# Filler matmuls on TensorE ahead of the last tiles of three layer norms

## The chip, the cores and the metric

One NeuronCore of one Trainium2 chip runs the program. The metric is the device time of one execution, in microseconds (us). TensorE (PE in the profile) multiplies, VectorE (DVE), ScalarE (ACT) and GpSimd (POOL) work on the data around it, and SyncE (SP) issues the loads.

## What is computed

Two layers, each a cross attention and then a mixture of experts, each behind a layer norm without weights and each added to the running x. There are 8 sequences of 56 tokens, 448 tokens of width 256, and a context of 8 x 1500 rows.

```python
x = x + _L0_xattn_ref(_layernorm(x), ctx_2048, ...)   # softmax attention, 16 heads of 128, 4 key heads
x = x + _L0_ffn_ref(_layernorm(x), ...)               # 8 experts of 176, top 2, and a shared one of 352
x = x + _L1_xattn_ref(_layernorm(x), ctx_2048, ...)   # linear attention: relu features of q and k, 16 heads of 16
x = x + _L1_ffn_ref(_layernorm(x), ...)               # 8 experts of 176, top 2, and a shared one of 704
```

## The kernel before

The program has three stages. `sums_and_queries` and `softmax_attention` fill the first 1046 us: they go through the context once for the key and value sums of the second layer and once for the softmax attention of the first. The third stage, `tail`, does everything that works on the 448 tokens, and the change lies in it alone.

In `tail` the tokens stand as four tiles of 112 (`TT` is 4, `TP` is 112), token by row, in `x`. One PSUM tensor, `bank`, has eight banks of 512 words. Each engine has its own list of instructions, written out by hand; semaphores order them across engines. The order on TensorE, with the lines that the prediction names:

1. `wo.turn_sums` and four calls of `wo.spread` (L1312): the softmax sums are spread over all partitions. One call is 8 matmuls. The weights of each are one column of `pick`, read 128 times (`pick[:, n:n + 1].to_broadcast([128, 128])`), the moving operand is `stack`, 128 x 112.
2. `wo.project`, four tiles (L102 to L104), with `ln1.turn` (L1213) of the tile before behind each. `turn(t)` waits for `xn_done`, transposes the two halves of one normalised tile and is read by ScalarE (`high` L1229, `copy` L1243), then by VectorE (`low` L1236).
3. `moe0.logits` (L1489: 16 instructions with 8 moving columns), then `moe0.tensor`: for each block of 128 hidden units `widen` (12 matmuls of 448 columns, L102 to L104), `spread` (L1524), `narrow` (L102 to L104, 256 columns). After two blocks TensorE turns the router's result (`turn_weights` L1512) and waits until ScalarE and VectorE have split it.
4. `ln2.turn` for four tiles, the queries (`lin.query` L1766) and features (L1779) of the linear attention, then `lin.read` (L1791: 16 instructions for one sequence, with 34 moving columns), `lin.turn` (L1803) and `lin.project` (L1815), with `ln3.turn` of the tile two back behind each.
5. `ln3.turn` of the last two tiles, `moe1.logits` (L1489) and `moe1.tensor`, built as in 3.

Behind `lin.project` VectorE adds the result to `x` (`lin.add` L1866, semaphore `lin.added`), takes mean and variance (L1173 to L1180), ScalarE computes a first reciprocal root (L1187, L1190), and VectorE sharpens it and writes the normalised tile into `scratch` (L1206, semaphore `xn_done`). ScalarE runs `ln3.guess` of tile 3 ahead of `high` and `copy` of tiles 2 and 3. `logits` of tile 0 waits until all four tiles went through `low`.

Of the kernel before, what the change touches and what calls it, by code (L numbers as in the profile page):

```python
# [18 lines left out]
TT = 4  # L19
TP = NTOK // TT  # L20
# [1862 lines left out]
def tail(nc, a, out, ident, kv, qT, qT_at, rz):  # L1883
# [8 lines left out]
    with ExitStack() as ctx:  # L1892
        p = Phase(nc, ctx, "tail")
        units = E * EU + SHARED1
        bank = p.ps("bank", [128, 8, 512])
# [24 lines left out]
        ln1, ln2, ln3 = (Norm(nc, p, f"ln{i}", x, xnT, xn, scratch, bank, banks, ident, zero)  # L1920
                         for i, banks in ((1, (6, 7, 0, 2)), (2, (0, 1, 2, 3)), (3, (0, 1, 2, 3))))
# [3 lines left out]
        wo = AttentionOutput(nc, p, x, qT, rz, a["wo0"], bank, ident)  # L1925
        lin = Readout(nc, p, kv, ln2, bank, ident, zero)
# [8 lines left out]
        @block.sync  # L1935
        def _(sp):
            wo.load(sp)
            sp.dma_start(x[:], a["x"].rearrange("(t p) d -> p t d", p=TP)).then_inc(x_loaded, 16)
            moe0.load_router(sp, a["router0"])
            moe1.load_router(sp, a["router1"])  # L1940
            moe0.load(sp, a["gate0"], a["up0"], a["down0"])
            lin.load(sp, room, a["wq1"], a["bq1"], a["wqf"], a["wo1"], a["bo1"])
            sp.wait_ge(moe0.w_lo, 3 * moe0.blocks)
            moe1.load(sp, a["gate1"], a["up1"], a["down1"])
            for t in range(TT):
                sp.wait_ge(moe1.added, t + 1)
                sp.dma_start(out[t * TP:(t + 1) * TP, :], x[:, t, :]).then_inc(stored, 16)
            sp.wait_ge(stored, 16 * TT)

        @block.tensor  # L1950
        def _(pe):
            wo.turn_sums(pe)
            for b in range(4):
                wo.spread(pe, b)
            for t in range(TT):
                for i in range(4):
                    wo.project(pe, t, i)
                    if t == 0 and i == 3:
                        wo.spread(pe, 4)
                        wo.spread(pe, 5)  # L1960
                    if t == 1 and i == 1:
                        wo.spread(pe, 6)
                        wo.spread(pe, 7)
                if t >= 1:
                    ln1.turn(pe, t - 1)
            pe.wait_ge(wo.scaled, 2 * B)
            ln1.turn(pe, TT - 1)
            for t in range(TT):
                moe0.logits(pe, t)
            moe0.tensor(pe)  # L1970
            for t in range(TT):
                ln2.turn(pe, t)
            lin.query(pe)
            lin.features(pe)
            for b in range(4):
                lin.read(pe, b)
            for t in range(TT):
                lin.turn(pe, t)
                lin.project(pe, t)
                if t + 2 < TT:  # L1980
                    lin.read(pe, 2 * t + 4)
                    lin.read(pe, 2 * t + 5)
                if t >= 2:
                    ln3.turn(pe, t - 2)
            for t in range(TT - 2, TT):
                ln3.turn(pe, t)
            for t in range(TT):
                moe1.logits(pe, t)
            moe1.tensor(pe)
# [213 lines left out]
```

## Time and profile before

| what | value |
|---|---|
| median of 3 runs | 1308.1 us (1306.59 to 1308.49) |
| the profiled execution, its own time | 1307.69 us |
| its span in the trace | 1306.0 us |
| busy: PE, DVE, ACT, POOL | 92%, 68%, 56%, 41% of the span |
| mean granted TensorE clock over the span | 0.963 of full speed |
| `tail`, from 1046 us to the end | 260 us |

The granted clock has two levels here: 1.00 is 2.4 GHz, 0.50 is 1.2 GHz. A row of the time line gives the start, how long the group was busy, engine, line, operation and tile, shape, and in brackets the idle time of that engine ahead of it and who ended it. In a time line a matmul's own duration holds its latency too; in a row that stands for a run of matmuls, the duration divided by the count is close to the step from one to the next. In the chain of waits a piece is only the part of the work that the end of the kernel had to wait for.

### The profile page before, as it was taken

The page shows a single profiled execution, that of the slowest core. Times are in us where ns is not written, and L with a number is a line of the kernel's source. Part 1 is how long each engine was busy: PE and PEld are TensorE (multiplying, and loading weights), DVE is VectorE, ACT ScalarE, POOL GpSimd, SP SyncE. Part 2 cuts the span into 40 slices and gives each one's busy share as a digit, 9 for nine tenths or more (in the row PEclk, how much of TensorE's full clock was granted, in tenths as well). Part 3 has the DMA queues.
Part 4 walks back from the last instruction along what each step waited for, and adds up shares of the span by engine and source line. Part 5 has one row for each costly group of instructions (what it writes and reads, how often), then busy time and mean ns, then how long its engine had stood idle before and what let it go on. Part 6 is the DMA issues. An engine that isn't in the chain of part 4 may idle for free. (4 is left out here: it accounts for less than half of the span.)

```text
span 1306.0 us, 27038 instructions
## 1 busy us (share of the span) xinstructions
PE 1199.6 (92%) x9589; PEld 1044.7 (80%) x9589; DVE 884.8 (68%) x1829; ACT 732.5 (56%) x1285; POOL 538.6 (41%) x559
## 2 busy tenths in 40 slices
PE   5999999999879999999999999999999876997798
PEld 4888888889758888888788887888878776785586
DVE  5666656566657887878887788778886465555554
ACT  4656556556545666576665666666656433442443
POOL 2423232232225363553545535445364063562242
PEclk9999999999988999999999999999999967997799
DMA  4211111110031111011110111101000070022000
GB/s 144 69 42 56 39 34 53 39 39 1 2 90 53 48 48 48 1 47 47 47 47 0 47 47 34 60 0 47 0 1 1 1 246 20 2 115 86 1 1 15
DMA packets 38795, 56.04 MB, mean 43 GB/s; under 512 B 3106, under 2 KB 37202, under 8 KB 38226
## 3 DMA queue, kind: packets, MB, share of 16 engines
q1 hardware_dynamic: 37922, 54.23, 13.1%
q10 hardware_dynamic: 816, 1.05, 0.3%
q8 instruction: 36, 0.59, 0.2%
q14 instruction: 21, 0.17, 0.0%
HBM read 54.81 MB, written 0.46 MB: 42 GB/s over the span
## 5 line engine op out<-in xcount | busy, mean ns | idle before, releaser
L1118 POOL TENSOR_TENSOR att_sq<-att_work,att_sq 128x500 fp32r<-128x500 f32 x90 | 119.8, 1331 | 159.7 <-DVE att_sq L1018 159.7
L1122 POOL TENSOR_TENSOR attention_kk<-att_work,attention_kk 128x500 fp32r<-128x500 f32 x90 | 122.1, 1357 | 153.3 <-DVE attention_kk L1026 153.3
L102 PE MATMUL att_csum<-att_pT,att_cn 125*128 125x448 f32 x384 | 156.3, 407 | 5.1 <-DVE att_pT L1067 4.4
L944 ACT ACTIVATE att_pr<-att_pr,att_nmx 112x1500 f32<-112x1500 f32 (+1 forms) x96 | 108.5, 1130 | 72.4 <-DVE att_nmx L1055 72.4
L104 PE MATMUL att_csum<-att_pT,att_cn 125*128 125x448 f32 x384 | 141.1, 367 | 0.0
L103 PE MATMUL att_csum<-att_pT,att_cn 125*128 125x448 f32 x384 | 140.0, 365 | 0.0
L535 DVE SCALAR_TENSOR_TENSOR attention_kk<-kvs_keys_ps,kvs_bk,attention_kk 64x500 fp32r<-64x500 f32 x96 | 70.8, 738 | 91.7 <-ACT attention_kk L419 90.1
L1067 DVE TENSOR_TENSOR att_pT<-att_ring,att_pT 125x448 fp32r<-125x448 f32 x192 | 118.3, 617 | 21.7 <-ACT att_pT L960 21.5
L1052 DVE TENSOR_SCALAR_CACHE_REDUCE att_pr<-att_ring 112x500 f32<-112x500 f32 x192 | 121.8, 675 | 6.4 <-PE att_ring L104 5.0
L290 PE MATMUL kvs_feat<-kvs_f,attention_kk 128*125 128x256 f32 x768 | 113.0, 284 | 10.9 <-DVE kvs_kp L607 10.1
L877 PEld LDWEIGHTS att_ring<-all_ident,att_pr 112*125 112x125 f32 x768 | 110.9, 190 | 14.4 <-ACT att_pr L944 2.2
L419 ACT ACTIVATE attention_kk<-kvs_keys_ps,kvs_bk 64x500 fp32r<-64x500 f32 x96 | 64.8, 675 | 92.3 <-PE kvs_keys_ps L104 91.0
L960 ACT ACTIVATE att_pT<-att_ring 125x448 fp32r<-125x448 f32 x192 | 102.5, 534 | 23.7 <-PE att_ring L877 23.7
L877 PE MATMUL att_ring<-all_ident,att_pr 112*125 112x112 f32 x768 | 111.6, 272 | 1.8 <-ACT att_pr L944 1.8
L290 PEld LDWEIGHTS kvs_feat<-kvs_f,attention_kk 128*125 128x125 f32 x768 | 98.5, 186 | 16.0 <-issue 14.1
L933 ACT ACTIVATE att_work<-att_proj,att_eps 128x500 f32<-128x500 f32 x90 | 60.8, 676 | 86.5 <-PE att_proj L104 86.5
L1021 DVE TENSOR_TENSOR att_work<-att_proj,att_work 128x500 f32<-128x500 f32 x90 | 60.9, 677 | 55.8 <-ACT att_work L940 55.4
L102 PE MATMUL att_ring<-attention_kk,attention_q 128*112 128x500 f32 x192 | 77.8, 405 | 17.5 <-DVE att_pr L1052 12.2
L472 ACT ACTIVATE kvs_kp<-kvs_feat,kvs_zero 125x512 f32<-125x512 f32 x96 | 65.9, 687 | 42.9 <-PE kvs_feat L290 42.4
L938 ACT ACTIVATE att_work<-att_mean,att_eps 128x500 f32<-128x500 f32 x90 | 61.1, 678 | 45.3 <-PE att_mean L835 45.3
L102 PEld LDWEIGHTS att_csum<-att_pT,att_cn 125*128 125x128 f32 x384 | 73.2, 191 | 15.1 <-DVE att_pT L1067 9.6
L1018 DVE CAST att_sq<-att_work 128x500 fp32r<-128x500 f32 x90 | 51.6, 574 | 39.8 <-ACT att_work L933 39.7
(279 smaller groups left out, 3276.9 us busy)
## 6 DMA issues: line engine op xcount, KB each, us to landing
attention_raw_t<-in_ctxT SPq DMA_DIRECT2D x45, 500.0 KB, 4.0
att_raw_n<-in_ctx SPq DMA_DIRECT2D x16, 750.0 KB
tail_gate_w<-in_gate SPq DMA_DIRECT2D x1, 2112.0 KB, 8.1
tail_up_w<-in_up SPq DMA_DIRECT2D x1, 2112.0 KB, 13.9
kvs_raw_q<-in_wq SPq DMA_DIRECT2D x8, 256.0 KB, 4.0
tail_wo_raw<-in_wo SPq DMA_DIRECT2D x4, 512.0 KB, 6.9
tail_down_w<-in_down SPq DMA_DIRECT2D x1, 2048.0 KB, 18.0
tail_gate_w<-in_gate SPq DMA_DIRECT2D x1, 1760.0 KB, 12.0
```

Source lines behind the costliest of these rows:

```text
L102: nc.tensor.matmul(out, w_lo, x_hi, start=start, stop=False, skip_group_check=True)
L103: nc.tensor.matmul(out, w_hi, x_lo, start=False, stop=False, skip_group_check=True)
L104: return nc.tensor.matmul(out, w_hi, x_hi, start=False, stop=stop, skip_group_check=True)
L290: last = nc.tensor.matmul(feat[0:KP, half, z], ks[:, c, 2 * half + g, y], f2[:, w, :], start=(w == 1), stop=(w == 0), skip_group_check=True)
L535: nc.vector.scalar_tensor_tensor(ks[64:128, c, 2 * m + h, :], keys_ps[y, 0:CH], bk[y, m:m + 1], ks[0:64, c, 2 * m + h, :].bitcast(F32), AL ...
L877: last = nc.tensor.transpose(ring[0:KP, t % 3, j * TP:(j + 1) * TP], pr[:, j, t * KP:(t + 1) * KP], ident[0:TP, 0:TP])
L944: nc.scalar.activation(pr[:, j, keys], pr[:, j, keys], ACT.Exp, scale=-1.0, bias=nmx[:, j:j + 1], accum_out=z[:, 4 * u + j, c:c + 1]).then ...
L960: nc.scalar.activation(pT[0][:, t % 3, :], ring[0:KP, t % 3, 0:QU], ACT.Copy).then_inc(pT_hi, 1)
L1052: nc.vector.tensor_scalar(pr[:, j, c * CH:(c + 1) * CH], ring[0:TP, c, 0:CH], -1.0, 3.0e38, ALU.mult, ALU.min, accum_out=mn[:, j, c:c + 1] ...
L1067: nc.vector.tensor_tensor(pT[1][:, t % 3, :], ring[0:KP, t % 3, 0:QU], pT[0][:, t % 3, :].bitcast(F32), ALU.subtract).then_inc(ring_free, 1)
L1118: nc.gpsimd.tensor_tensor(sq[1][:, i % 2, :], work[:, i % 2, :], sq[0][:, i % 2, :].bitcast(F32), ALU.subtract).then_inc(sq_lo, 1)
L1122: nc.gpsimd.tensor_tensor(kk[:, c, 2 + gi, :], work[:, i % 2, :], kk[:, c, gi, :].bitcast(F32), ALU.subtract).then_inc(k_lo, 1)
```

## The change

A helper `steady(n, count)` issues `count` equal matmuls into bank `n`, 112 columns each, with the operands of `wo.spread`: the first column of `pick`, read 128 times, and `stack`. Nobody reads the result, and no semaphore is raised. It is called four times on TensorE: 36 matmuls ahead of the last tile of the first norm, 44 ahead of the four tiles of the second, and 10 and 16 ahead of tiles 2 and 3 of the third. Ahead of the 10 TensorE waits until `lin.added` is 4, the number of tiles.

```diff
         @block.tensor
         def _(pe):
+            def steady(n, count):
+                for _ in range(count):
+                    nc.tensor.matmul(bank[:, n, 0:TP], wo.pick[:, 0:1].to_broadcast([128, 128]),
+                                     wo.stack[:], start=True, stop=True, skip_group_check=True)
+
             wo.turn_sums(pe)
...
             pe.wait_ge(wo.scaled, 2 * B)
+            steady(3, 36)
             ln1.turn(pe, TT - 1)
             for t in range(TT):
                 moe0.logits(pe, t)
             moe0.tensor(pe)
+            steady(7, 44)
             for t in range(TT):
                 ln2.turn(pe, t)
...
-            for t in range(TT - 2, TT):
-                ln3.turn(pe, t)
+            pe.wait_ge(lin.added, TT)
+            steady(7, 10)
+            ln3.turn(pe, TT - 2)
+            steady(7, 16)
+            ln3.turn(pe, TT - 1)
             for t in range(TT):
                 moe1.logits(pe, t)
             moe1.tensor(pe)
```

How the order on TensorE changes at the first norm, between the end of the attention's projection and the router's logits of the first mixture (- before, + changed):

```order
 L104 MATMUL tail_bank<-tail_wo_7144,tail_o_7146 112x256
-L1213 MATMUL tail_bank<-all_ident,tail_scratch 128x112 x4
+L1213 MATMUL tail_bank<-all_ident,tail_scratch 128x112 x2
+L1954 MATMUL tail_bank<-tail_stack,tail_pick 128x112 x36
+L1213 MATMUL tail_bank<-all_ident,tail_scratch 128x112 x2
 L1489 MATMUL tail_bank<-tail_moe_router,tail_xnT 112x8 x8
```

The 36 matmuls stand between the transposes of tile 2 and those of tile 3. They have no wait of their own but the one on `wo.scaled`, which stood there already.

The same at the third norm, behind the last projection of the linear attention:

```order
 L1815 MATMUL tail_bank<-tail_lin_wo,tail_attT 112x256 x2
-L1213 MATMUL tail_bank<-all_ident,tail_scratch 128x112 x6
+L1213 MATMUL tail_bank<-all_ident,tail_scratch 128x112 x2
+L1954 MATMUL tail_bank<-tail_stack,tail_pick 128x112 x10
+L1213 MATMUL tail_bank<-all_ident,tail_scratch 128x112 x2
+L1954 MATMUL tail_bank<-tail_stack,tail_pick 128x112 x16
+L1213 MATMUL tail_bank<-all_ident,tail_scratch 128x112 x2
 L1489 MATMUL tail_bank<-tail_moe_router,tail_xnT 112x9 x8
```

Here 10 matmuls and the new wait stand ahead of the transposes of tile 2, and 16 ahead of those of tile 3; the transposes of tile 1 keep their place. The other engines' lists are unchanged.

## Rows read from the trace of the kernel before

**Rows 1.** The page's second part: TensorE's granted clock in 40 slices.
```profile
PEclk9999999999988999999999999999999967997799
```

**Rows 2.** Chain of waits in the tail: start us, us, engine, tile, line.
```profile
1104.39 3.12 PE tail_bank L1489 x16
...
1181.33 5.22 PE tail_bank L1766 x8
...
1189.90 4.34 PE tail_bank L1791 x64
...
1214.41 0.42 DVE tail_scratch L1206
...
1214.88 0.65 PE tail_bank L1213 x2
...
1216.79 3.13 PE tail_bank L1489 x16
```

**Rows 3.** Stretches of the tail: from:to, length, PE busy (count), PEclk, DMA share, GB/s.
```profile
1048.20:1055.10 6.90, 6.90 (x32) 0.50 1.02 306
...
1097.20:1099.90 2.70, 0.00 (x0) 1.00 0.57 140
1100.10:1110.20 10.10, 6.41 (x26) 0.50 0.06 20
1114.20:1116.50 2.30, 0.00 (x0) 1.00 0.00 0
1117.20:1120.40 3.20, 3.20 (x9) 0.50 0.00 0
1175.20:1185.20 10.00, 5.62 (x14) 0.50 0.84 286
...
1192.20:1198.90 6.70, 6.10 (x47) 0.50 0.01 2
1199.10:1209.10 10.00, 7.72 (x76) 1.00 0.00 1
1209.30:1222.80 13.50, 7.28 (x28) 0.50 0.01 2
```

**Rows 4.** Time line of PE: the spreading of the softmax sums, at either clock.
```profile
1048.14 7.08 PE L1312 MATMUL tail_bank<-tail_stack,tail_pick 128*128 128x112 f32 x32 [1.50 <-DVE tail_stack L1357]
...
1068.60 1.89 PE L1312 MATMUL tail_bank<-tail_stack,tail_pick 128*128 128x112 f32 x16
1070.33 0.33 PE L102 MATMUL tail_bank<-tail_wo,tail_o 128*112 128x256 f32 x1
```

**Rows 5.** Time line of PE at the first norm, and behind it.
```profile
1102.51 0.61 PE L1213 MATMUL tail_bank<-all_ident,tail_scratch 112*128 112x112 f32 x2 [5.36 <-DVE tail_scratch L1206]
...
1108.27 0.57 PE L104 MATMUL tail_bank<-tail_xn,tail_wide 128*128 128x448 f32 x1
...
1111.20 0.37 PE L102 MATMUL tail_bank<-tail_xn,tail_wide 128*128 128x448 f32 x1
```

**Rows 6.** Time line of PE and DVE at the second norm, and reading at full clock.
```profile
1179.00 1.75 PE L1213 MATMUL tail_bank<-all_ident,tail_scratch 112*128 112x112 f32 x8 [5.55 <-DVE tail_scratch L1206]
...
1178.54 1.39 DVE L1206 TENSOR_SCALAR tail_scratch<-tail_x,tail_ln_mv,tail_ln_rstd 112x256 f32<-112x256 f32 x4
...
1180.80 0.39 DVE L1249 COPY tail_xnT<-tail_bank 128x224 f32<-128x224 f32 x1 [0.35 <-PE tail_bank L1213]
...
1201.81 1.84 PE L1791 MATMUL tail_bank<-tail_kvd,tail_qf 128*56 128x34 f32 x32
```

**Rows 7.** Time line of PE, DVE and ACT at the third norm.
```profile
1208.01 0.41 PE L1213 MATMUL tail_bank<-all_ident,tail_scratch 112*128 112x112 f32 x2 [0.16 <-DVE tail_scratch L1206]
1211.81 0.64 PE L1213 MATMUL tail_bank<-all_ident,tail_scratch 112*128 112x112 f32 x2 [3.38 <-DVE tail_scratch L1206]
...
1211.67 0.41 DVE L1866 TENSOR_TENSOR tail_x<-tail_x,tail_bank 112x256 f32<-112x256 f32 x1
...
1213.51 0.34 ACT L1229 ACTIVATE tail_xn<-tail_bank 128x224 fp32r<-128x224 f32 x1
```

## The prediction

> **What bounds the kernel now.** I read the page first. The granted clock of TensorE is full nearly everywhere; the slices that are not lie at the start of the softmax stage and in the tail, the last 260 us [rows 1]. Then the chain of waits in the tail: TensorE's own work is on it, with the router's logits (3.12 us), the queries (5.22 us) and the reading (4.34 us), and in between stands the chain of a layer norm, VectorE's write of the last normalised tile and the transposes behind it [rows 2]. Third, the granted clock in stretches of the tail: after each wait for a norm TensorE is at 0.50, and what follows the wait runs so until the clock returns: to 1110.2 behind the first norm, to 1185.2 behind the second, to 1222.8 behind the third [rows 3]. So the tail pays twice for a norm, once for the wait and once for the slow start behind it. The change adds work into the waits and takes none away; it can gain by the clock alone.
>
> **The filler's price.** Its matmuls have the shapes and operands of the ones that spread the softmax sums. At half clock 32 of those took 7.08 us, 0.221 us each. At full clock 16 took from 1068.60 to 1070.33, 0.108 us each [rows 4]. These two prices carry the sum. I count nothing for other engines: the filler writes a bank that nobody reads then, raises no semaphore and moves no instruction of theirs.
>
> **First norm, 36 matmuls.** TensorE is idle for 5.36 us up to 1102.51 [rows 5], so from 1097.15. The clock is still full there (1.00 to 1099.9, then 0.50) [rows 3]. 36 x 0.108 = 3.9 us, done at 1101.05, 1.4 us ahead of the transposes: hidden. Were all at half clock it would be 36 x 0.221 = 8.0 us and the transposes 2.6 us late; that is the upper end. What it can give: the transposes 0.2 us (0.61 as in rows 5 against 0.41 at full clock, rows 7), the logits about half of 3.12 us [rows 2], and about seven matmuls of the first hidden block, which took 0.57 us and not 0.37 [rows 5], 1.4 us. Together 3.2 us, the lower end. I take 0.2. Between the filler's end and the hidden block there are still 1.4 us of idling, one pair of transposes, 1.3 us of idling until the last tile is split (1103.1 to 1104.39), and then the narrow logits. An idle gap of 2.30 us alone was enough at 1114.2: from 1117.2 the clock was 0.50 although TensorE worked again [rows 3]. So the fall comes some us later, but ahead of the work that it hurts.
>
> **Second norm, 44 matmuls.** The idle time is 5.55 us up to 1179.00 [rows 6], and 44 x 0.108 = 4.75 us end at 1178.2: hidden; if the last ten met half clock it would be 1.1 us more, 0.3 us late. Of the queries' 5.22 us some 3.9 ran at half clock, until 1185.2 [rows 2, 3]; at full clock they would save 1.95 us. The start of the queries could come 0.4 us earlier and no more, since VectorE writes the four tiles from 1178.54 to 1179.93 and copies two of them behind that (0.39 us each) [rows 6]. So the bounds are 2.4 us gained and 0.3 lost. I take nothing: from the filler's end to the queries at 1181.33 TensorE idles 0.8 us, transposes for 1.75 us and idles 0.5 us again, and the eight transposes ran at 0.50 from first to last [rows 3, 6]. The fall would move from 1175 to about 1178 or to the queries' start, and the queries would begin slow as they do now. The Trainium skill, "TensorE: Matmul & The Clock Gate", section "Part 4: PE-mode transpose", says the same more sharply: transposes do not count as activity in the way matmuls do. By that rule the pause behind the filler is 3.1 us long; the rows show that transposes did not raise the clock, not that they cannot hold it.
>
> **Third norm, a wait and 26 matmuls.** Here the filler does not begin when TensorE falls idle. It waits for the last addition to x, which ends at 1212.08 [rows 7]. TensorE's work before that ends at 1208.42, so 3.7 us of idling stay unfilled, and the clock is 0.50 from 1209.3 to 1222.8 [rows 3, 7]. All 26 then run at half clock unless they raise it, and the 32 of the same kind in a row did not: it was 0.50 over the whole stretch [rows 3, 4]. Worked out: 1212.1 + 10 x 0.221 = 1214.3, the two transposes of tile 2 at the same step 0.44, 1214.7, then 16 x 0.221 = 3.54, so the transposes of tile 3 start at 1218.3. They start at 1214.88 now, 0.05 us after VectorE finished the tile [rows 2]: **3.4 us late**. Queued behind the new wait are the transposes of tile 2; ScalarE takes that tile at 1213.51 [rows 7] and would at 1214.9, 1.4 us late, which the 3.4 of tile 3 cover. ScalarE and VectorE wait for tile 3, the logits for both, and all further work for the logits; nothing else can run meanwhile. At full clock the cost would be 1212.1 + 26 x 0.108 + 0.2 = 1215.1, 0.25 us. Bounds for the place: 3.4 lost, or, with the clock up as well, see the first rival.
>
> **Sum.** -0.2 + 0 + 3.4 = +3.2 us. The profiled execution took 1307.69 us and would take 1310.9; the median of the runs stands 0.4 above it, so 1311.3 us.
>
> **Rivals.**
> 1. *The filler counts as work, so the clock holds and rises.* The first norm then gives 3.2 us, the second 2.4. At the third the filler starts at half clock and raises it after some 3 us, about what the hidden block needed, from the logits' end at 1219.9 to 1222.8 [rows 2, 3]: the 10, the transposes and two of the 16 are slow (2.9 us), the other 14 take 1.5, so tile 3 is turned at 1216.5, 1.6 us late, and transposes, logits and block gain 0.2 + 1.6 + 1.4. Net -1.6. In all -7.2: 1300.9 us, faster. For it: the mix at 1068 to 1070, where 16 such matmuls among projections ran at full clock [rows 4]. Against: the 6.9 us at 0.50 [rows 3], and the pauses left behind each filler. It decides from the point where the clock is 1.00 at the logits. The Trainium skill, the same page, section "Why this matters for your kernels", advises to keep TensorE busy without pause so that the clock comes up and stays up; by that rule this rival would be the forecast. The row with 32 matmuls disagrees.
> 2. *The second norm alone pays.* The rest of the pause, with the transposes in it, is short enough to hold the clock into the queries. 3.2 - 2.4 = +0.8: 1308.9 us, no measurable change. The fall at 1117 came after 2.3 us of idling, and here no single idle piece is longer than 0.8 us; against it stand the slow transposes.
> 3. *The clock is lost later and costs more.* If it falls with the queries and comes back later than 1185.2, the 1.3 us of them that ran at full clock double, and so may the first 2.3 us of the reading (1189.9 to 1192.2): +3.6 more, 1314.9 us. For it: the reading at 0.50 from 1192.2 to 1198.9 although TensorE was busy 6.10 of 6.70 us [rows 3] shows that these narrow matmuls neither hold nor raise the clock soon; at full clock 32 of them took 1.84 us [rows 6] where 64 took 4.34 [rows 2]. Against: the mean effect of a moved fall can as well be a gain.
> 4. *The filler of the third norm is cheap*, because it meets full clock after all: +0.25 - 0.2, 1308.2 us. Against it: the 3.7 us of idling in front.
>
> **Chances.** Forecast 0.55 (its own range 1310 to 1313), rival 1 0.09, rival 2 0.18, rival 3 0.14, rival 4 0.04. About 0.2% (2.6 us, so 1305.5 to 1310.7) is what a measurement of this kernel can tell from no change. Most of the forecast's share lies above it, 0.46, with rival 3 that makes 0.60 for slower; 0.09 of it with rivals 2 and 4 makes 0.31 for the same; rival 1 is the 0.09 for faster. The range takes in rivals 2 to 4 and leaves out rival 1: 1307.8 to 1315.2.
>
> **What the profile after would show.** Right: the filler in two prices, 0.108 us a piece at the first two norms, 0.221 at the third; PE at 0.50 at both routers' logits and at the start of the queries; the last transposes of the third norm starting 3.4 us later, counted from the last addition, and waiting for nobody. The prediction is wrong if the clock stands at 1.00 when the logits or the queries begin, if the 26 matmuls take less than 5 us, or if the time from the last addition to the logits grows by less than 3 us.

## The result

| | before | changed |
|---|---|---|
| median of 10 runs each | 1307.43 us (1305.67 to 1310.1) | 1310.95 us (1309.67 to 1312.1) |
| the profiled execution, its own time | 1307.69 us | 1309.67 us |
| its span | 1306.0 us | 1308.0 us |

The changed kernel takes 1.0026 of the time before, 95% interval 1.0016 to 1.0036: 3.4 us more, 2.1 to 4.7. The forecast was 1311.3 us. Two slow executions are left out of the comparisons below: one of 2931 us of the kernel before, and one of 1361 us, at a granted clock of 0.839, of the last experiment's kernel.

### The profile page after: what moved, and what is told of

It reads as the page before. It is cut to its first block and busy times, and to the rows that moved or that the text cites. A ratio compares the mean times of both kernels' runs of the same rounds, so it can differ in the third digit from the quotient of the medians.

```text
span 1308.0 us, 27249 instructions
## 1 busy us (share of the span) xinstructions
PE 1215.5 (93%) x9695; PEld 1061.3 (81%) x9695; DVE 883.8 (68%) x1829; ACT 731.9 (56%) x1285; POOL 538.0 (41%) x559
## 5 line engine op out<-in xcount | busy, mean ns | idle before, releaser
L290 PEld LDWEIGHTS kvs_feat<-kvs_f,attention_kk 128*125 128x125 f32 x768 | 99.1, 187 | 15.4 <-issue 14.1
```

Source lines behind the costliest of these rows:

```text
L290: last = nc.tensor.matmul(feat[0:KP, half, z], ks[:, c, 2 * half + g, y], f2[:, w, :], start=(w == 1), stop=(w == 0), skip_group_check=True)
```

## The profile after

The granted clock in 40 slices, of the page (compare rows 1). The last eight slices, the tail, read 6 7 9 9 7 7 9 9 before and 7 7 9 9 6 7 9 9 now: higher ahead of the first mixture, lower between the two mixtures.

```profile
PEclk9999999999989999999999999999999977996799
```

The chain of waits in the tail of the changed kernel (start, length, engine, tile, line), which answers to rows 2. L1954 is the filler.

```profile
1102.25 3.13 PE tail_bank L1489 x16
...
1177.28 1.40 PE tail_bank L1213 x8
...
1179.24 3.25 PE tail_bank L1766 x8
...
1185.83 5.14 PE tail_bank L1791 x64
...
1211.18 2.38 PE tail_bank L1954 x10
1213.56 0.41 PE tail_bank L1213 x2
1213.97 3.32 PE tail_bank L1954 x16
1217.29 0.42 PE tail_bank L1213 x2
...
1218.98 3.12 PE tail_bank L1489 x16
```

The logits cost what they did (3.13, 3.12). The queries shrank from 5.22 to 3.25 us, the first four sequences of the reading grew from 4.34 to 5.14. And the filler of the third norm stands in the chain itself, with 2.38 and 3.32 us: work without a result has become what the end of the kernel waits for. The fillers of the first two norms are not in the chain.

TensorE in stretches of the tail (from:to, length, busy and count, granted clock, DMA), which answers to rows 3:

```profile
1095.80:1099.20 3.40, 3.40 (x32) 1.00 0.62 179
1101.90:1108.40 6.50, 6.15 (x25) 0.50 0.00 0
1171.80:1176.60 4.80, 4.79 (x43) 1.00 1.01 400
1177.40:1186.90 9.50, 7.39 (x53) 1.00 0.46 146
1187.20:1193.00 5.80, 5.20 (x47) 0.50 0.00 0
1193.00:1211.00 18.00, 16.16 (x95) 0.50 0.01 1
1211.20:1217.20 6.00, 6.00 (x29) 0.50 0.00 0
1217.20:1227.90 10.70, 9.42 (x35) 0.50 0.00 1
```

Three things are to be seen. At the first norm the clock is full under the filler and at half behind it. At the second it is full through filler, transposes and queries, up to 1187. Then it falls in the reading and does not come back for 41 us, through the whole reading, the third norm and its filler, until the second hidden block of the second mixture.

The time between marks that both traces have, in us. A mark is the start of the first instruction of its kind; of the additions named as last or final it is the start of that one.

| stretch | before | changed | difference |
|---|---|---|---|
| first norm: last addition to logits | 7.40 | 7.12 | -0.28 |
| logits to the mixture's first addition | 68.39 | 68.82 | +0.43 |
| mixture's first addition to queries | 8.55 | 8.17 | -0.38 |
| queries to reading | 8.57 | 6.59 | -1.98 |
| reading to last addition | 21.77 | 24.89 | +3.12 |
| third norm: last addition to logits | 5.12 | 8.26 | +3.14 |
| logits to the last tile's final addition | 84.78 | 84.55 | -0.23 |

The sum is +3.8 us. The span grew by only 2.0, since in this pair of executions the stages before the tail were 1.86 us quicker in the changed kernel (the addition that opens the table starts at 1095.13 and not 1096.99), where no instruction was changed; the medians do not rest on that pair. The +0.43 of the first mixture is not an effect that I can show: in kernels with nothing changed up to there the same stretch took 68.39 to 68.70 us.

## Experiments

Theory: the third norm's wait and 26 half-clock matmuls cost the whole; the second norm's gain is given back in the reading; the first gives 0.3. Rivals: the lost clock in the reading is the cost, or filler is dear wherever it stands, or the new wait is. Each kernel below was timed against the kernel before on the same chip. The edits are shown against the kernel before, and cut short: added lines and some neighbours.

### One place at a time

```diff
 # e1_first: only this
+            steady(3, 36)
 # e2_second: only this
+            steady(7, 44)
 # e3_third: only these
+            pe.wait_ge(lin.added, TT)
+            steady(7, 10)
             ln3.turn(pe, TT - 2)
+            steady(7, 16)
             ln3.turn(pe, TT - 1)
 # e4_third_wait: only this
+            pe.wait_ge(lin.added, TT)
```

> Only the 36 filler matmuls of the first norm; the other two places as before. Theory (the third norm's filler costs 3.1 to 3.4 us, the first only shortens the transposes of its tile): 0.2 to 0.3 us faster than before, which cannot be told from no change; last addition of the first norm to the logits 7.1 us against 7.4 before, clock 0.50 at the logits. Rival (the filler holds the clock into the logits): 3 us faster. Other rival (any filler delays its norm): slower.

> Only the 44 filler matmuls of the second norm. Theory: the clock stays full through the queries, which take 3.3 us and not 5.2, so the queries gain 2.4 us with their earlier start, and the reading behind them loses most of it because the clock then falls in the reading and stays down until the third norm; in all between 1.5 us faster and 1.5 us slower. Rival A (the change is slower because of this lost clock): 3 us slower or more. Rival B (the second norm's filler pays in full): 2.4 us faster.

> Only the wait and the 26 filler matmuls of the third norm. Theory: all of the change's cost is here, 3.1 to 3.4 us slower than before; filler at 0.22 us each, clock 0.50; last addition to the logits 7.8 us against 4.7. Rival (the cost lies in the reading, by the second norm's filler): no more than 1 us slower.

> Of the whole change only the wait for the last addition ahead of the third norm's last two tiles, no filler anywhere. Theory: within 0.2 us of before, since the transposes of tile 2 move by 0.3 us and ScalarE takes that tile 1.4 us later anyway. Rival (the wait makes the transposes of tile 2 late and that is passed on): 0.3 to 1.5 us slower.

| kernel | ratio to before | 95% interval |
|---|---|---|
| first norm's filler alone | 0.9997 | 0.9985 to 1.0010 |
| second norm's filler alone | 0.9996 | 0.9985 to 1.0007 |
| third norm's wait and filler alone | 1.0021 | 1.0008 to 1.0033 |
| third norm's wait alone | 1.0004 | 0.9993 to 1.0015 |

Only the third norm's part is slower, by 2.8 us (1.0 to 4.3). The three parts add up to 1.0014, with an error of some 0.002 from their intervals, which agrees with the whole change's 1.0026. In the third part's profile the last addition to the logits took 8.26 us, as in the changed kernel (the expectation's 7.8 counts from the addition's end, 0.4 us later). The clock was at half all the while, and ahead of it through the reading but for its first 2 us (time in stretches, then the time line of TensorE):

```profile
1192.00:1229.00 37.00, 33.09 (x177) 0.50 0.00 1
```
```profile
1214.04 2.38 PE L1954 MATMUL tail_bank<-tail_stack,tail_pick 128*128 128x112 f32 x10 [0.69 <-DVE tail_x L1866]
...
1216.51 3.64 PE L1954 MATMUL tail_bank<-tail_stack,tail_pick 128*128 128x112 f32 x16
```

The wait alone is not told from nothing: the same stretch is 5.12 us with it, to the hundredth what it was. So what is dear is the filler behind the wait.

The second norm's filler alone shows both halves of its effect. TensorE in two stretches of that kernel:

```profile
1179.30:1188.90 9.60, 7.49 (x54) 1.00 0.45 143
1189.10:1226.40 37.30, 31.30 (x177) 0.50 0.00 1
```

Mixture to queries 8.17, queries to reading 6.59 (2.36 us gained), and reading to last addition 24.92 for 21.77 (3.15 lost). The runs give no measurable change, so the rival that this lost clock is the cost falls, and so does the one that the queries' gain is kept. One caution: in the profile of the third part alone the reading took 24.14 us though nothing before it was changed. When the clock comes back within the reading, as it did at 1199 in the kernel before [rows 3], differs from one execution to the next, and how much of the 3.1 us is owed to the filler ahead I cannot fully separate. What the traces give: of the eight profiled kernels in which nothing between the second norm and the end of the reading was changed, six took 21.77 to 21.80 us from the reading to the last addition, this one 24.14 and the wide filler at the first norm (below) 19.05; the two with the narrow filler at the second norm and none in the reading took 24.89 and 24.92.

### The same filler without the wait, and a wider one

```diff
 # e5_third_early
+            steady(3, 28)
             ln3.turn(pe, TT - 2)
+            steady(3, 20)
             ln3.turn(pe, TT - 1)
 # e6_third_wide: 448 columns, 41 rows
+            def wide(n, count):
+                for _ in range(count):
+                    nc.tensor.matmul(bank[:, n, 0:NTOK], member[:, 0:128], combT[:], start=True, stop=True)
+            wide(3, 15)
             ln3.turn(pe, TT - 2)
+            wide(3, 10)
             ln3.turn(pe, TT - 1)
+            wide(5, 5)
 # e7_first_wide
+            pe.wait_ge(moe0.member_done, 2)
+            wide(3, 24)
             ln1.turn(pe, TT - 1)
+            wide(3, 5)
```

> Third norm alone: the same narrow filler without the wait for the last addition, so that it begins when TensorE falls idle: 28 ahead of tile 2, 20 ahead of tile 3, into bank 3. Theory (the filler was dear because it began after the clock had fallen): the filler runs at 0.108 us each, the transposes of tile 3 start no more than 0.2 us later than before, the clock still falls behind the filler; within 1 us of before, against 2.8 us slower for the third norm's filler with its wait. Rival (narrow filler cannot hold the clock from where it stands after the last projection): the 48 run mostly at 0.22 us and cost 4 us or more.

> Third norm alone, no wait, filler of 448 columns (the operands of the spreading of the routing weights): 15 ahead of tile 2, 10 ahead of tile 3, 5 behind it. Theory (wide filler holds the clock and raises it if it had fallen): 0.20 us each at full clock, 0.50 only shortly if at all, logits 1.6 us and not 3.1, the first hidden block at full clock: 2 to 3 us faster than before. Rival (any pause and the narrow logits bring the clock down whatever fills the rest): no gain, within 0.5 us.

> First norm alone, 24 fillers of 448 columns ahead of the last tile and 5 behind it. Theory: clock 1.00 from the projection into the hidden blocks, last addition to the logits 7.1 us, logits 1.6 us and not 3.1, 3 us faster than before. Rival (the narrow logits bring it down): the logits partly at half clock, 0.3 to 1 us faster. The data of the moving operand are zero here; if zeros do not count as work, the clock falls as before and the gain is 0.3 us.

Without the wait 48 fillers cost nothing that can be measured where 26 cost 2.8 us: ratio 1.0001 (0.9983 to 1.0019), last addition to logits 4.90 us and not 8.26. The two intervals overlap a little; it is the profile that tells them apart. TensorE's time line and its stretches in that kernel:

```profile
1208.60 3.31 PE L1954 MATMUL tail_bank<-tail_stack,tail_pick 128*128 128x112 f32 x28
1212.22 0.41 PE L1213 MATMUL tail_bank<-all_ident,tail_scratch 112*128 112x112 f32 x2 [0.31 <-DVE tail_scratch L1206]
1212.40 2.42 PE L1954 MATMUL tail_bank<-tail_stack,tail_pick 128*128 128x112 f32 x20
...
1216.99 3.12 PE L1489 MATMUL tail_bank<-tail_moe_router,tail_xnT 128*112 128x9 f32 x16 [1.28 <-DVE tail_xn L1236]
```
```profile
1208.70:1211.90 3.20, 3.20 (x30) 1.00 0.00 0
1212.50:1214.70 2.20, 2.20 (x22) 1.00 0.00 0
1215.80:1216.40 0.60, 0.00 (x0) 1.00 0.00 0
1216.50:1223.20 6.70, 6.21 (x25) 0.50 0.01 4
```

The same instruction in the same place is half the price, and the clock was never lost ahead of it. The clock is lost in the pause of 1.3 us behind the last tile, just ahead of the logits, so the gain is still missing.

The wide filler failed its theory. At the third norm: ratio 1.0019 (1.0008 to 1.0030), slower, with last addition to logits at 6.85 us for 5.12. At the first: 0.9994 (0.9984 to 1.0005), with last addition to logits at 9.71 us for 7.40. The stretches at the third norm, then at the first:

```profile
1207.90:1211.10 3.20, 3.20 (x16) 1.00 0.00 0
1212.20:1218.00 5.80, 5.80 (x16) 0.50 0.00 0
```
```profile
1098.00:1100.70 2.70, 2.70 (x14) 1.00 0.52 126
1100.90:1114.40 13.50, 13.50 (x44) 0.50 0.06 18
```

With four times the columns a matmul the clock falls at 1212 and stays at half while TensorE is busy without a gap. At the first norm it fell at 1100.8, in the middle of an unbroken row of 24. There the moving data were zeros; at the third norm they were the first mixture's routing weights, so zeros are not the whole reason. What the two share against the narrow filler, which held, is their operands: 41 of 128 rows used and not all, 448 columns and not 112, and other weights. I take the rows for the likely cause; that is not shown.

### The pause ahead of the reading

```diff
 # e8_second_read: with the 44 of the second norm; e11_read_only: without them
             lin.features(pe)
+            pe.wait_ge(moe1.member_done, 2)
+            pe.wait_ge(lin.f_act, 1)
+            wide(2, 7)
```

> Second norm alone with its 44 narrow fillers, and 7 fillers of 448 columns in the pause of 1.5 us ahead of the reading. Theory (the pause together with narrow reading lets the clock fall): the reading begins at full clock and keeps it longer, 4.9 us from the reading to the last addition come back if it holds to the end; 2 to 5 us faster than before. Rival (the narrow reading alone brings it down): the clock falls in the reading all the same, 1 us faster to 1 us slower.

> No filler at the norms; only 7 fillers of 448 columns and 41 rows in the pause of 1.5 us ahead of the reading. Theory (the 4.3 us gained with the second norm's filler and this one come from the reading alone): queries 5.2 us as before, reading to the last addition 19.1 us and not 21.8, 2.7 us faster than before. Rival (it takes both): within 1 us of before.

Ratios 0.9964 (0.9950 to 0.9977) with the second norm's filler and 0.9964 (0.9951 to 0.9977) without: 4.7 us faster, by seven matmuls. In both profiles reading to last addition is 19.07 us for 21.77, at full clock throughout. TensorE in the kernel with those seven alone:

```profile
1176.80:1186.60 9.80, 5.62 (x13) 0.50 0.83 280
1187.00:1210.40 23.40, 17.97 (x190) 1.00 0.00 1
```

2.7 us of the 4.7 are in this pair of profiles. Part of the rest fits the caution above: of the 22 executions of the kernel before that the seven alone were compared with, six show a mean granted clock of 0.958 and took 1311.2 to 1312.1 us, while none of the 20 with the seven fillers fell below 0.965 or took more than 1306.9 us. That the six lost their clock in the reading was not shown run by run.

The theory that narrow reading brings the clock down by itself is refuted: with the pause ahead of it filled it held from 1191.4 to 1210.4, 19 us. But an empty pause of 1.5 us does not always bring it down either. In the profile of the wide filler at the first norm the reading began at 1193.84 behind an empty pause of 1.53 us and ran at full clock to its end:

```profile
1189.60:1209.20 19.60, 15.88 (x181) 1.00 0.01 1
```

That kernel's runs fit this: its first norm grew by 2.31 us in the profile, and yet it took no longer than the kernel before (0.9994). So a single profile cannot show what the seven fillers do. That rests on the two ratios, and on both profiles reading 19.07 where six of eight without them read 21.8.

### Filler with all rows and 224 columns, in every pause

```diff
+            def firm(n, count, operand):
+                for _ in range(count):
+                    nc.tensor.matmul(bank[:, n, 0:2 * TP].rearrange("p (c n) -> p c n", n=TP),
+                                     wo.pick[:, 0:1].to_broadcast([128, 128]), operand,
+                                     start=True, stop=True, skip_group_check=True)
+            tile0 = xn[0][:, :, 0:TP]
 # e9_third_firm
+            pe.wait_ge(ln3.x_hi, 1)
+            firm(3, 28, tile0)
             ln3.turn(pe, TT - 2)
+            firm(3, 22, tile0)
             ln3.turn(pe, TT - 1)
+            firm(5, 10, tile0)
 # e10_all_firm: that, 46 and 10 around the first norm's last tile (behind ln1.x_hi),
 # 44 and 4 around the second norm's tiles, 12 ahead of the reading (behind lin.f_act)
 # e12_all_firm_route: that, and behind turn_weights of each mixture
+            firm(6, 17, tile0)      # moe0; 12 for moe1
```

> Third norm alone, filler from the moment TensorE is idle, with 128 rows and 224 moving columns (two halves of a normalised tile): 28 ahead of tile 2, 22 ahead of tile 3, 10 behind it. Theory (the 41-row filler of 448 columns failed for its few rows, the 112-column one leaves a pause behind tile 3): 0.11 us each as the weights' load sets the step, clock 1.00 through the filler, logits 1.6 us, first hidden block at full clock: 2.5 to 3 us faster than before. Rival (the narrow logits bring the clock down all the same): logits partly or all at half clock, within 1 us of before.

> The 224-column filler in every pause: 46 and 10 around the last tile of the first norm, 44 and 4 around the second norm's tiles, 12 ahead of the reading, and the third norm as in the run before. Theory: the clock stays 1.00 from the first projections to the end but for the wait for the routing weights: 3 us at the first norm, 2.4 at the queries, 3 to 4 in the reading, 3 at the third norm, so 8 to 12 us faster than before. Rival (narrow reading and logits bring it down wherever they are): 3 to 5 us faster, as with the filler ahead of the reading alone.

> As the run with filler in every pause, and 17 and 12 more of the same filler while TensorE waits for the split routing weights of the first and of the second mixture. Theory: the falls at 1114 and 1219 of that run, 6.8 us at half clock each in a dense stretch, go away; each costs up to 3.4 us, so 4 to 6 us less than there, 14 to 16 us faster than before. Rival (the fall is not due to this pause, or the filler delays the routing weights' spreading): no change against that run, 10 us faster than before.

| kernel | ratio to before | 95% interval |
|---|---|---|
| third norm | 0.9982 | 0.9969 to 0.9995 |
| every pause of norms and reading | 0.9921 | 0.9904 to 0.9938 |
| and the two waits for the routing weights | 0.9868 | 0.9845 to 0.9891 |

At the third norm (time line of TensorE, then its stretches):

```profile
1208.35 3.36 PE L1959 MATMUL tail_bank<-tail_xn,tail_pick 128*128 128x224 f32 x28
...
1216.75 1.71 PE L1489 MATMUL tail_bank<-tail_moe_router,tail_xnT 128*112 128x9 f32 x16 [0.16 <-DVE tail_xn L1236]
```
```profile
1208.40:1215.00 6.60, 6.18 (x54) 1.00 0.01 2
1215.30:1216.50 1.20, 1.20 (x12) 1.00 0.00 0
1216.80:1226.40 9.60, 7.44 (x45) 1.00 0.00 1
```

The step of a filler is 0.11 us, as with half the columns (28 took 3.36 us here and 3.31 us there, each with the last one's latency); the logits take 1.71 us for 3.12 and what follows them is at full clock. With every pause filled two falls were left, at the waits for the routing weights:

```profile
1113.70:1120.40 6.70, 6.70 (x17) 0.50 0.01 2
1120.50:1219.40 98.90, 93.24 (x672) 1.00 0.19 67
1219.50:1226.30 6.80, 6.80 (x16) 0.50 0.00 0
```

The last kernel fills those too, and there is no fall left from the first norm to 1290, near the end of the second mixture (the clock in its trace is full from 1094.4 to 1292.3):

```profile
1097.00:1290.00 193.00, 186.05 (x1231) 1.00 0.11 39
```

It takes 1294.08 us (median) against 1310.51 of the kernel before on the same chip, 17 us less (14 to 20): faster than both kernels. By its marks: first norm to logits 7.16, first mixture 64.18 (for 68.39), to the queries 8.17, queries to reading 6.59, reading to last addition 19.06, third norm to logits 4.90, second mixture 80.43 (for 84.78): 14.1 us in the profiled pair. The other 3 us of the medians are not found in any stretch; the profiled execution of the kernel before, 1307.7 us, is one of its faster ones. TensorE does 205 more matmuls than before for it.

## Why the prediction was right, and where it was not

**The filler's price** held: 36 in 3.9 us were forecast for the first norm, and TensorE stood idle 1.29 us before the last tile, 1.4 forecast; at the third norm 10 took 2.38 us and 16 took 3.32 in the chain, 0.22 each on average.

**First norm** held: 0.2 us forecast, 0.28 found, hidden as worked out, and the clock at half at the logits (3.13 us). The runs with this part alone (0.9997) cannot tell 0.3 us from nothing.

**Third norm** held, mechanism and size: 3.4 us forecast, 3.14 found between the last addition and the logits, 2.8 (1.0 to 4.3) in the runs with that part alone. The forecast was too high by 0.3 us in two prices: the filler's step was 0.217 and not 0.221 us, and the two transposes of tile 2 held TensorE for 0.29 us and not 0.44. That the cause is the start behind the lost clock, and not filler as such, is shown by the version without the wait. Tile 2, 1.4 us late by the forecast, was hidden behind tile 3 as said. With 6.00 us of filler at 0.50 rival 4, cheap filler here, fell too.

**Second norm: the step that failed.** "I take nothing ... the queries would begin slow as they do now." The queries began and ended at full clock: 3.25 us for 5.22, and 0.38 us earlier, as the forecast's bound on the side of gain had it (2.36 found, 2.4 given). I read the eight transposes at 0.50 as a sign that they cannot hold the clock; they ran at half clock because it was lost before them. With the clock up they took 1.38 us and it stayed. By the forecast's own test, "wrong if the clock stands at 1.00 when the logits or the queries begin", it was wrong here: right in time, wrong in what happens at the queries. The Trainium skill, "TensorE: Matmul & The Clock Gate", section "Part 4: PE-mode transpose", says that transposes do not count as activity the way matmuls do. This trace shows full clock across them and can neither confirm the rule nor refute it: counted without them the pause from the filler to the queries was 2.65 us (1.27 us idle, 1.38 us of transposes), and no run changes the transposes alone.

**What made the total right all the same** is rival 3's mechanism, which I had kept apart from rival 2. The clock fell later, in the reading, and stayed down for 41 us, +3.12 us in that stretch. Rivals 2 and 3 came together, -2.4 and +3.1, and left the second place at +0.8 in the profile and at nothing measurable alone (0.9996). The term of the forecast, nothing, was right by this cancelling and not by its reason: at this place the total was luck. How firmly the +3.1 belongs to the filler is as uncertain as said at the experiments.

**Rival 1** fell as stated: 6.00 us of the third norm's filler ran at 0.50 and did not raise the clock. The Trainium skill, "TensorE: Matmul & The Clock Gate", section "Why this matters for your kernels", advises to keep TensorE busy continuously to get to full clock, and to leave no long idle gaps. The last version, with its pauses filled and 17 us gained, agrees; those 6.00 us of filler and transposes without a gap, all at 0.50, do not, and neither does the clock lost in a pause of 1.3 us ahead of the logits. The 17 us are no measure of rival 1 and its 7.2 us, which priced the three norms of this change; they come also from the reading (2.7 us in the profiled pair) and from the waits for the routing weights.

## What to carry to other kernels

In these runs filler on TensorE paid where it began while the clock was still full and left next to no pause before the work it was to help; the one here that waited for another engine's result first began after the fall, ran at twice the price and pushed the critical tile back. Follow the chain of pauses to the work that is to gain. Filling the last pause ahead of it paid alone (4.7 us ahead of the reading); filling an earlier one, with a pause still open behind it, moved the fall into the next stage and gained nothing. Read the granted clock stretch by stretch behind every wait, also in stages that the edit does not touch, and in more than one execution before a stretch is charged to an edit.

## What the runs showed of the hardware

- A filler of 448 columns on 41 rows did not hold the clock: it fell in the middle of an unbroken row of 24 (first norm, at 1100.8) and stayed at half while TensorE was busy without a gap (third norm, 5.80 of 5.80 us at 0.50), where one of 112 columns on 128 rows held it for 5.7 us. Seven of the wide ones, 1.4 us, ran at full clock. Which property decides, rows, columns or the operand, was not tried by itself.
- The 112-column filler held a full clock (5.7 us) but did not raise a half one (the 32 like it, 6.90 us busy without a gap at 0.50 [rows 3], and the third norm's, 6.00 us).
- With weights of 128 columns a filler costs nearly the same with 112 and with 224 moving columns: 28 took 3.31 and 3.36 us at full clock.
- With seven fillers in a pause of 1.5 us the clock was full over the next 19 us, the reading with its matmuls of 34 columns and the projections between them, in both profiled kernels that had them. Without them it was at half clock for 6.7 us of the reading [rows 3], for nearly all of it, or, in one profiled kernel, not at all: the same instructions behind the same pause do not always get the same clock.
